# Second experts: outputs read back before the last three tiles, which are added by scatters to rows of their own

## The reference, cut to what matters

```python
def _L1_ffn_ref(x, w_fc, w_proj, w_gate):          # x: layer norm of h; H, NE, K = 768, 8, 2
    router_probs = softmax(einsum('btc,ce->bte', x, w_gate))
    top_p, top_i = top_k(router_probs, K)
    top_p = top_p / sum(top_p)
    ...  # h = gelu(x @ w_fc[:, :, e]), o = h @ w_proj[:, :, e] for the two experts e in top_i
    return einsum('btck,btk->btc', o, top_p)
h = h + _L1_ffn_ref(_layernorm(h), ...)
```

## Time and profile before

| | |
|---|---|
| median of the runs | 588.76 us |
| the profiled execution | 594.99 us, its span 593.2 us |
| TensorE | 492.7 us busy (83%) |
| VectorE | 319.5 us (54%) |
| ScalarE | 206.6 us (35%) |
| GpSimd | 154.6 us (26%) |
| DMA | 84.86 MB, mean 143 GB/s |

### The profile page before, as it was taken

One profiled execution on the slowest core, in us unless ns is written; L12 is line 12 of the kernel. 1 busy time (PEld: TensorE's weight loads), 2 busy tenths in 40 slices (PEclk: granted clock), 3 DMA queues, 4 the chain that ended last, 5 costly groups with the idle time before them and its releaser, 6 DMA issues.

```text
span 593.2 us, 12427 instructions
## 1 busy us (share of the span) xinstructions
PE 492.7 (83%) x4370; PEld 456.0 (77%) x4371; DVE 319.5 (54%) x1037; ACT 206.6 (35%) x441; POOL 154.6 (26%) x148
## 2 busy tenths in 40 slices
PE   3999999988514676899999679768999999999960
PEld 3999997568513565899999666758999999999950
DVE  1567999778999887322222466793222222222207
ACT  3630013857993357044343152261111121211110
POOL 1493000000001000555533300006544434443120
PEclk9999999989557667799999889879999999999995
DMA  8995100000006422387775497023666556667018
GB/s 302 411 339 152 51 1 1 0 3 2 0 1 220 129 106 108 84 217 179 180 171 109 108 277 306 1 107 98 202 204 184 168 166 187 183 183 209 28 52 294
DMA packets 40659, 84.86 MB, mean 143 GB/s; under 512 B 7270, under 2 KB 23186, under 8 KB 39586
## 3 DMA queue, kind: packets, MB, share of 16 engines
q1 hardware_dynamic: 33218, 72.81, 38.1%
q0 software_dynamic: 7392, 11.41, 8.5%
HBM read 70.33 MB, written 13.86 MB: 142 GB/s over the span
## 4 chain that ended last, share of the span: by engine, by line
PE 69%; DVE 17%; DMA 5%; ACT 4%; issue 2%; SPq 1%; POOL 0%; ACTq 0%; DVEq 0%; POOLq 0%
PE ps L1136 19%; PE ps L1112 13%; PE ps L886 13%; PE ps L1120 7%; DVE h L1923 2%; PE ps L1001 2%; DMA arena<-tok_w 1%; PE ps L1103 1%; PE ps L973 1%; DVE xT L1770 1%; PE ps L974 1%; PE ps L866 1%; PE ps L867 1%; DVE arena L1624 1%; DVE arena L1485 1%
## 5 line engine op out<-in xcount | busy, mean ns | idle before, releaser
L1136 PE MATMUL ps<-arena,xn 128*128 x696 | 123.1, 327 | 2.1 <-ACT xn L776 2.1
L1136 PEld LDWEIGHTS ps<-arena,xn 128*128 128x128 f32 x696 | 111.8, 190 | 4.2 <-issue 3.9
L514 POOL DMA_INDIRECT xT<-rows,from_i x58 | 56.3, 971 | 164.0 <-DVE from_i L1784 118.9
L886 PE MATMUL ps<-arena 128*128 128x192 f32 (+1 forms) x588 | 85.4, 333 | 10.2 <-DMA arena<-x_strips 9.2
L529 POOL DMA_INDIRECT made<-xT,to_i x58 | 67.9, 1170 | 99.2 <-DVE xT L1822 65.7
L886 PEld LDWEIGHTS ps<-arena 128*128 128x128 f32 (+1 forms) x588 | 83.3, 194 | 10.9 <-ACT arena L555 8.9
L1112 PE MATMUL ps<-xn,arena 128*128 128x128 f32 x696 | 88.0, 277 | 0.0
L1112 PEld LDWEIGHTS ps<-xn,arena 128*128 128x128 f32 x696 | 86.1, 194 | 0.1
L779 ACT ACTIVATE xn<-ps 128x384 f32<-128x384 f32 x78 | 32.6, 493 | 141.3 <-PE ps L1122 114.9
L1810 DVE COPY xn<-ps 128x128 f32<-128x128 f32 x58 | 16.9, 292 | 117.2 <-PE ps L1104 114.8
L776 ACT ACTIVATE xn<-ps,b_all 128x128 f32<-128x128 f32 x114 | 30.8, 390 | 62.6 <-PE ps L1122 51.0
(11 more groups left out here) (373 smaller groups left out, 771.1 us busy)
## 6 DMA issues: line engine op xcount, KB each, us to landing
arena<-ffn_a SPq DMA_DIRECT2D x58, 384.0 KB, 3.9
arena<-ffn_b SPq DMA_DIRECT2D x116, 96.0 KB, 4.4
arena<-x_blocks SPq DMA_DIRECT2D x16, 384.0 KB, 6.7
arena<-x_strips SPq DMA_DIRECT2D x3, 1536.0 KB, 12.3
arena<-ffn SPq DMA_DIRECT2D x4, 1152.0 KB, 15.5
rows<-xn SPq DMA_DIRECT2D x8, 384.0 KB, 2.3
arena<-made SPq DMA_DIRECT2D x8, 384.0 KB, 6.2
arena<-tok_w SPq DMA_DIRECT2D x8, 288.0 KB, 7.4
```

The source lines that it names most:

```text
L514: pool.indirect_dma_start(sx[:, k % 6], None, F["src"], bass.IndirectOffsetOnAxis(from_i[:, k:k + 1], 0)).then_inc(sem(f"sx_in{k % 6}"), 16)
L886: mm = pe.matmul(sum_ps(name, j), xs[rows, strip, 2 * j + b, 128 * c:128 * c + 128], w[rows], start=(name, j // 2) not in opened, stop=lef ...
L1136: mm = pe.matmul(ps[:, result_bank(k, N), 0:DIM], hT[:, u % 2, 128 * c:128 * c + 128], F["w2"][:, bass.ds(e2 + DIM * c, DIM)], start=(c == ...
```

## The change

`LATE = 3`. The rows of `made1` are set to zero early in the program, and the readback of all 4096 rows waits only for the scatters of tiles 0 to 35. The last three tiles (36, 37, 38) don't go to `made1`, so their rows read as zeros. Their results are multiplied by the row's share on VectorE as they leave PSUM, and scattered with addition to `late`: the first 2048 + 256 rows of `made0`, free by then, set to zero in the middle of F1; the row is the token's number (`late_i`). A token can have both of its rows in these tiles, so each of the three scatters waits until the one before has landed. `late` is then read in 4 pieces and added to h, each addition for four token blocks, and h is stored in 4 pieces. The shares of the late rows are gathered from DRAM, where a DMA puts `pk` (now laid out token, then choice) in the middle of F1. The buffer of the readback moves in SBUF, since the down weights of F1 are still in use when it fills. Some semaphores are shared by events that had one each (`ones_row`, `gate_set` and `wnat_set` become `pool_set`, `tok_b_in` becomes `cst_in`, `b2_in` becomes `ffn_in0`).

```diff
-STORES = ((0, 4), (4, 8), (8, 12), (12, 14), (14, 16))
+STORES = ((0, 4), (4, 8), (8, 12), (12, 16))
+LATE = 3
+        late = made0[0:TOKS + 256, :]
+        shares = rows0.rearrange("r (c o) -> (r c) o", o=1)
-        got = [h[:], view(0, [2 * NTOK, DIM])]
+        lin_at = E1 * HCH * DIM
+        got = [h[:], view(lin_at, [2 * NTOK, DIM])]
+        got_late = view(lin_at + 2 * NTOK * DIM, [NTOK, DIM])
...
+            sp.wait_ge(sem("pool_set"), 2)
+            sp.dma_start(made1[0:2 * TOKS, :].rearrange("(k p) c -> p k c", p=128),
+                         pbc[:, 0, :].unsqueeze(1).to_broadcast([128, 2 * NTOK, DIM])).then_inc(sem("made_set"), 16)
...
+                    if n and k == 12:
+                        late_set()
+            def late_set():
+                sp.wait_ge(sem("shares"), 1)
+                sp.dma_start(shares[0:2 * TOKS, :].rearrange("(p k) c -> p (k c)", p=128),
+                             pk[:].rearrange("p t s -> p (t s)")).then_inc(sem("shares_out"), 16)
+                sp.wait_ge(sem("pool_set"), 6)
+                sp.dma_start(late[0:TOKS + 128, :].rearrange("(k p) c -> p k c", p=128),
+                             pbc[:, 0, :].unsqueeze(1).to_broadcast([128, NTOK + 1, DIM])).then_inc(sem("made_set"), 16)
...
-                    sp.wait_ge(sem(f"y_st{n}{u}"), 16 * ((F["tiles"] + 2 - u) // 3))
+                    sp.wait_ge(sem(f"y_st{n}{u}"), 16 * ((F["tiles"] - LATE * n + 2 - u) // 3))
...
+            for u in range(3):
+                sp.wait_ge(sem(f"y_st1{u}"), 16 * ((TILES1 + 2 - u) // 3))
+            for i in range(4):
+                r = slice(4 * i, 4 * i + 4)
+                sp.wait_ge(sem("h_sum"), i + 1)
+                sp.dma_start(got_late[:, r, :], late[0:TOKS, :].rearrange("(b t) c -> b t c", t=NTOK)[:, r, :]).then_inc(sem(f"back_{i}"), 16)
...
-                for k in range(N):
+                pool.wait_ge(sem("made_set"), 64)
+                for k in range(N - LATE * n):
...
+                    if n and k == 14:
+                        pool.wait_ge(sem("shares_out"), 16)
+                        for x in range(LATE):
+                            pool.indirect_dma_start(share[:, x:x + 1], None, shares,
+                                                    bass.IndirectOffsetOnAxis(to_i[:, N - LATE + x:N - LATE + x + 1], 0)
+                                                    ).then_inc(sem("share_in"), 16)
             exchange(F0)
+            pool.memset(pbc[:, 0, :], 0.0).then_inc(sem("pool_set"), 1)
             exchange(F1)
+            pool.wait_ge(sem("made_set"), 80)
+            for k in range(TILES1 - LATE, TILES1):
+                pool.wait_ge(sem("y_out1"), k + 1)
+                if k > TILES1 - LATE:
+                    pool.wait_ge(sem(f"y_st1{(k - 1) % 3}"), 16 * ((k - 1) // 3 + 1))
+                pool.indirect_dma_start(late, bass.IndirectOffsetOnAxis(late_i[:, k - TILES1 + LATE:k - TILES1 + LATE + 1], 0), yo[:, k % 3],
+                                        None, compute_op=ALU.add).then_inc(sem(f"y_st1{k % 3}"), 16)
...
+            dve.wait_ge(sem("made_set"), 32)
             row, top = pbc[r3, 1, :], low[r3, 0, 0:96].bitcast(BF16)
...
+                if n:
+                    tail = slice(N - LATE, N)
+                    link(dve.tensor_scalar(pad, row[:, tail], -0.75, cst[:, C_P + 1:C_P + 2], ALU.is_lt, ALU.mult))
+                    dve.tensor_tensor(late_i[:], from_i[:, tail], pad, ALU.add)
...
+            def weighted(start, end):
+                for i in range(start, end):
+                    dve.wait_ge(sem(f"back_{i}"), 32 if i < 4 else 16)
+                    for s in range(2):
+                        for t in range(2 * i, 2 * i + 2):
+                            ins = dve.scalar_tensor_tensor(h[:, t, :], got[1][:, 2 * t + s, :], pk[:, t, s:s + 1], h[:, t, :], ALU.mult, ALU.add)
...
+                        ins = dve.tensor_scalar(yo[:, u % 3], ps[:, result_bank(k, N), 0:DIM], share[:, x:x + 1], None, ALU.mult)
...
+                        if n and isinstance(k, int) and k + 3 == N:
+                            dve.wait_ge(sem("share_in"), 16 * LATE)
+                            weighted(0, (0, 0, 1)[b])
                         result(k + b, u + b, j)
...
+            weighted(1, 8)
+            dve.wait_ge(sem("h_sum"), 8)
+            for i in range(4):
+                dve.wait_ge(sem(f"back_{i}"), 48)
+                r = slice(4 * i, 4 * i + 4)
+                dve.tensor_tensor(h[:, r, :], h[:, r, :], got_late[:, r, :], ALU.add).then_inc(sem("h_final"), 1)
```

More of the change, by code:

```diff
@@ L183, in build @@
         te_i = sb("te_i", [1, 4, 40], I32)
-        pk = sb("pk", [128, 2, NTOK])
+        pk = sb("pk", [128, NTOK, 2])
+        late_i = sb("late_i", [128, LATE], I32)
+        share = sb("share", [128, LATE])
+        late = made0[0:TOKS + 256, :]
+        shares = rows0.rearrange("r (c o) -> (r c) o", o=1)
         xnf = xn[:].rearrange("p a b -> p (a b)")
@@ L478, in link @@
                 pool.wait_ge(sem("pool_step"), steps[0])
[L481 to L482 removed]
+            pool.memset(xT1[K1:128, :], 1.0).then_inc(sem("pool_set"), 1)
+            pool.wait_ge(sem("pool_set"), 1)
             link(pool.memset(wnat[96:128, 5:7, :], 0.0))
+            link(pool.memset(pbc[:, 0, :], 0.0))
             for w in gate_w1:
[L485 to L487 removed]
+                pool.memset(w[K1:128], 0.0).then_inc(sem("pool_set"), 1)
+            pool.memset(wnat[64:128, 4, :], 0.0).then_inc(sem("pool_set"), 1)
+            pool.wait_ge(sem("pool_set"), 4)
             pool.wait_ge(sem("w_row"), 1)
@@ L1463, in _ @@
             token_row(1)
-            dve.wait_ge(sem("wnat_set"), 1)
+            dve.wait_ge(sem("pool_set"), 4)
             dve.wait_ge(sem("wnat_in"), 128)
@@ L1794, in route @@
                 dump, none = rt[:, 1280:1280 + N], g
+                pad = rt[:, 1324:1324 + LATE]
                 link(dve.tensor_scalar(dump, cst[:, C_TILE:C_TILE + N], 128.0, cst[:, C_P + 1 + n:C_P + 2 + n], ALU.mult, ALU.add))
                 link(dve.scalar_tensor_tensor(none, row, -0.75, dump, ALU.is_lt, ALU.mult))
+                if n:
+                    tail = slice(N - LATE, N)
+                    link(dve.tensor_scalar(pad, row[:, tail], -0.75, cst[:, C_P + 1:C_P + 2], ALU.is_lt, ALU.mult))
+                    dve.tensor_tensor(late_i[:], from_i[:, tail], pad, ALU.add)
                 dve.scalar_tensor_tensor(to_i[:, 0:N], row, 0.5 * n, none, ALU.add, ALU.add).then_inc(sem("places"), 1)
                 if n:
-                    dve.wait_ge(sem("soft_exp"), 1)
+                    dve.wait_ge(sem("exp_out"), 2)
                     link(dve.tensor_scalar(c16, d16, 1.0, None, ALU.add))
-                    link(dve.reciprocal(pk[:, 0, :], c16))
-                    dve.tensor_tensor(pk[:, 1, :], d16, pk[:, 0, :], ALU.mult)
+                    link(dve.reciprocal(pk[:, :, 0], c16))
+                    dve.tensor_tensor(pk[:, :, 1], d16, pk[:, :, 0], ALU.mult).then_inc(sem("shares"), 1)
+            def weighted(start, end):
[4 more added lines that the diff above has]
+                            ins = dve.scalar_tensor_tensor(h[:, t, :], got[1][:, 2 * t + s, :], pk[:, t, s:s + 1], h[:, t, :], ALU.mult, ALU.add)
+                        if s == 0:
+                            link(ins)
+                    ins.then_inc(sem("h_sum"), 1)
             def copies(F):
@@ L1820, in result @@
                         ins = dve.tensor_tensor(yo[:, u % 3], ps[:, result_bank(k, N), 0:DIM], b2_all[:, bass.ds(e, DIM)], ALU.add)
+                    elif isinstance(k, int) and k >= N - LATE:
+                        x = k - N + LATE
+                        ins = dve.tensor_scalar(yo[:, u % 3], ps[:, result_bank(k, N), 0:DIM], share[:, x:x + 1], None, ALU.mult)
                     else:
@@ L1892, in _ @@
             link(dve.tensor_tensor(ltmp[:, 0:16], ps[:, 6, 0:16], cst[:, C_SEL:C_SEL + 16], ALU.mult))
-            dve.tensor_reduce(stat[:, 500:501], ltmp[:, 0:16], AX.X, ALU.add).then_inc(sem("gate_logit"), 1)
+            dve.tensor_reduce(stat[:, 500:501], ltmp[:, 0:16], AX.X, ALU.add).then_inc(sem("exp_in"), 1)
             plus_normed(12, 16)
-            dve.wait_ge(sem("gate_exp"), 1)
+            dve.wait_ge(sem("exp_out"), 1)
             link(dve.tensor_scalar(stat[:, 502:503], stat[:, 501:502], 1.0, None, ALU.add))
@@ L1918, in _ @@
             copies(F1)
-            for i in range(8):
-                dve.wait_ge(sem(f"back_{i}"), 32 if i < 4 else 16)
-                for s in range(2):
-                    for t in range(2 * i, 2 * i + 2):
-                        ins = dve.scalar_tensor_tensor(h[:, t, :], got[1][:, 2 * t + s, :], pk[:, s, t:t + 1], h[:, t, :], ALU.mult, ALU.add)
-                    if s == 0:
-                        link(ins)
-                ins.then_inc(sem("h_final"), 1)
+            weighted(1, 8)
[4 more added lines that the diff above has]
```

(1 more changed line is left out.)

40 lines of the change are left out of this document (19 added, 21 removed).

## The result

The changed kernel is slower: its median is 598.78 us (four runs, 595.76 to 600.19) against 589.88 for the kernel before (four runs); the ratio on record is 1.0107 with a 95% interval of 1.0062 to 1.0152. Run again later, twelve times, it gave 1.0093 [1.0064, 1.0121], or 5.5 us, against 592.29 for 35 runs of the kernel before (588.74 to 595.64). The forecast was 591.0 us with a range up to 594.8. The ratios are the record's own and are not the quotients of the medians, which would be 1.0151 and 1.0110; the runs of one kernel spread over 6 to 8 us, so I go by the ratios and their intervals.

A forecast was written before the change was run, and what follows sets the result against it. The matrix engine holds 69% of the chain, but only the last 20 us can move: 7 us hidden, a serial late chain added, span 595.4 against 593.2. 588.76 + 2.2 = 591.0 us, range 587.5 to 594.8.

The forecast's parts named there:

- step 2: End chain: three adding scatters in a row, first 6.4 us, then 3.5 each; sum taken 14.0, bounds 11.1 to about 17.
- The base: The 2.2 us difference of spans was put on 588.76 us, the median of the runs of the kernel before.
- What goes: End: readback waits only for tile 35's scatter and the weighted additions end earlier, a gain of 7 us were nothing added.
- Step 1, the start: New end chain starts with tile 36's scatter at 569.67; multiplying by the share instead of copying was charged nothing.
- Steps 3 to 5, readback, addition, store: End: late readback of four pieces 7.05 us, last addition 0.96, last store 3.2, then 0.4 to the end.
- Saturated: End transfers saturate: first scatter 7.8 us, second 5.3, last store 4.7; 595.7 us, chance 0.18.
- Hardly felt: End scatters hardly feel the readback, 3.5 us each, store lands in 2.7; -1.2 us, 587.6 us, chance 0.17.
- short end: In addition to hardly felt, late readback lands 1.3 us sooner, store in 1.9; -3.3 us, 585.5 us, chance 0.06.
- VectorE keeps GpSimd out: End: 28 back-to-back two-input additions block generation of scatters 37 and 38 until 583.4; 598.0 us, chance 0.06.
- Weights of tile 12: Second experts: matrix engine waits for tile 12's weights behind the second zeroing, 3 us on top of 2.2; 594 us, chance 0.05.

The follow-up runs named there:

- b2: Changed kernel without its late path (three adding scatters, late readback, last four additions); the last three tiles' results are left out of the output: ratio 0.9887, tail 17.1 us.
- a2: Changed kernel without the two zeroings and the waits for them; output sums rows not set to zero: ratio 1.0051 against the kernel before, tail 27.9 us.
- a1: The changed kernel run once more with no edit: ratio 1.0093 against the kernel before, tail 28.5 us.
- a3: Changed kernel without the chain of waits, each late tile adding to rows of its own, only one set read back: ratio 0.9954, tail 21.3 us.
- a4: Changed kernel with readback pieces 4 to 7 held until tile 36's scatter has landed: ratio 1.0079 against the kernel before, tail 27.4 us.
- c2: Changed kernel with two sets of late rows, both read back, and readback pieces 4 to 7 held until tile 36's scatter landed: ratio 1.0017, tail 25.9 us.
- c1: Changed kernel with tile 37 adding to a second set of rows, tile 38 waiting for tile 36's scatter alone, both sets read back: ratio 1.0057, tail 26.6 us.
- b3: Changed kernel with two late tiles instead of three, weighted additions all behind the last result: ratio 1.0053 against the kernel before, tail 26.1 us.
- b4: Changed kernel with its three late scatters writing instead of adding, the chain of waits kept: ratio 1.0032 against the kernel before, tail 25.5 us.
- b1: Kernel before with only the two zeroings, the settings of the zero row and the waits for them added: ratio 0.9999, tail 24.2 us.
- c3: Changed kernel with one late tile instead of three, so no chain of scatters: ratio 1.0041 against the kernel before, tail 27.1 us.

## Why the prediction was wrong

Two terms failed: the landing of the first late scatter in step 2, and the base that the forecast was added to. I go through its own steps, taken from tile 36's result to the end of the span. The forecast for this stretch was 26.5 us, measured were 28.8.

- **What goes: right.** The readback left 2.4 us behind tile 35's scatter, and the additions were hidden. Worth 7 by the forecast, 6.7 by b2's ratio.
- **Step 1, the start: 0.4 too low.** From tile 36's result to its scatter's issue took 1.18 us, before 0.76. The multiplication by the share costs hardly more than the copy, as assumed (0.42 against 0.36 us); the rest goes with the added wait on GpSimd. In a2, where that wait is gone and the multiplication stays, it is 0.70.
- **Step 2, three scatters: the step that failed, 2.9 too low.** The first was taken at 6.4 us by the row with the nearest share of busy engines, and took 8.20 (7.96 and 7.93 in a1 and a2). This is above even the upper bound of 7.8. The share was no guide: over the three scatters of 5.3, 6.4 and 7.8 us it was 0.91, 0.93 and 0.93. And the one of 7.8, issued at 310.38, had no packet moved for its first 5.3 us, which the trace of before could have shown. The rows with 5.3 to 7.8 lay beside loads of weights, this one beside eight pieces of 384 KB issued within 3.7 us. The two gaps between a landing and the next issue were taken at 0.3 us and took 0.75 and 0.72, 0.9 together. The quiet scatters, 3.5 each, were right (3.66 and 3.56). The sum of the step, 16.9, lies within its own bounds (11.1 to about 17), but the range of the forecast did not carry them along.
- **Steps 3 to 5, readback, addition, store: 0.9 too high.** Forecast 11.7 us from the third landing to the end, measured 10.8: the late readback with its issue took 5.5 and not 7.1, the additions behind its last piece 1.9 and not 0.96, the store with what follows 3.3 and not 3.6.
- **The sum.** 0.4 + 2.9 - 0.9 gives 2.4 more than forecast, 2.3 measured. It makes 4.5 us of tail against before; the ratio says 5.5 (3.8 to 7.2 by its interval). The 1.0 between them isn't explained, and lies inside the interval.
- **The base.** The forecast was put on 588.76, the median of three runs. In 35 runs the median is 592.29. That is 3.5 us, more than the error of the sum, and the range had nothing in it for this. The error of the sum alone would have left the time at 593.3, within the range. The 7.8 us between 591.0 and the measured median of 598.78 are 3.5 of base, 2.3 of the sum, the unexplained 1.0, and 1.0 by which the medians (598.78 and 592.29) differ more than the ratio says.

The rivals. *Saturated* was the nearest: it had the first scatter at 7.8 and the cause, the full transfer beside it, and asked 6.9 of tail where 4.5 came, since it let the second scatter and the store suffer too, which they didn't. *Hardly felt* and *short end* are refuted by 8.20. *VectorE keeps GpSimd out* is refuted: GpSimd took 1.69 and 1.56 us for its scatters in the middle of and behind 28 additions back to back, and 1.61 for the one ahead of them; in a3, with both beside them, 1.58 and 1.56. The rule of the Trainium skill, SBUF — State Buffer, section Who interferes with whom, had no effect here that these rows show. *Weights of tile 12* is refuted by the matrix engine's busy time, 163.00 of 163.00. Its sum has a slip: 10.6 us grown by half from 437.3 give 453.2, 0.1 too late, not 453.8.

The first scatter again. The rows show three sizes for one adding scatter of 98 KB: 3.6 with nothing beside it, 4.0 and 4.3 beside what is left of half a readback (a4, c2), 6.8 to 8.2 beside a full one; 5.9 and 6.5 beside four pieces issued with it (c1, a4) lie between. That the readback makes it long is shown (a4), and that it doesn't have to run to its end first (b3). That the time goes in front of and between its packets and not in them is shown by the queues (1.2 MB first, then 76 ns a packet against 107 alone), and b4's writing scatter took 7.17 too, so reading back for the addition isn't most of it. What holds the first packet back that long, these runs don't show.

The Trainium skill, DMA: Bandwidth & Descriptors, section Queues, rings and completion order, has the engines take turns between queues by packet. Once the scatter's packets have begun, both queues do run side by side (186 and 144 packets from 571.34 to 574.60). But the prediction drew from it that the scatter waits for a packet or two and could be nearer 5, and said that the trace agrees. It does not: 442 packets of the readback came first, some 28 on each engine, and the measured 8.20 decides against the size. The scatter of 310.38 had told as much before the change.

## What to carry to other kernels

Moving a transfer ahead of its last inputs pays only if what finishes those inputs is short and not serial: here 7 us were hidden and 11.7 paid, of which having each adding scatter wait for the one before made 7.5 to 8.2. Price a small indirect transfer beside a deep readback at twice what it takes alone (7 to 8 us for 3.6 here), even though it doesn't wait for the readback's end, and look in the view of the queues when its first packet moves; holding part of the readback back only hands the delay to the next link of the chain. And before a forecast of half a per cent is put on a median, look at how far the runs spread: three were too few here by more than the effect.

## What the runs showed of the hardware that was not expected

**The same stretches take one of a few lengths.** The kernels are identical up to the second experts but for the small parts named, and yet the stretch of the first experts, from the first gather to the readback, took 97.0 us in before, a2, a3 and b4 (96.7 and 96.8 in c1 and c2), and 95.0 to 95.2 in after, a1, a4, b1, b2, b3 and c3. The stretch behind it, to the first store of normed rows, took 48.7 to 49.2, 50.3 to 50.6 or 52.4 to 52.8. The windows show what differs: the granted clock, first of before, then of after, at the same two places.

```profile
245.00:255.00 10.00, 9.74 (x85) 9.20 (x84) 2.29 (x9) 3.01 (x12) 5.27 (x6) 0.85 0.56 164
345.00:355.00 10.00, 6.90 (x46) 6.58 (x45) 5.39 (x37) 4.39 (x10) 0.00 (x0) 0.83 1.07 264
```

```profile
244.63:254.63 10.00, 9.74 (x97) 9.23 (x96) 2.65 (x10) 3.29 (x13) 5.29 (x6) 1.00 0.75 193
343.00:353.00 10.00, 7.53 (x65) 7.08 (x64) 6.45 (x41) 4.81 (x11) 0.00 (x0) 1.00 1.08 272
```

In before the clock was at its upper level for only part of these windows, in after for all of them, and in the first place as many busy us hold 85 matmuls in the one and 97 in the other. This is why the two profiled spans differ by 0.8 us only (593.2 and 594.0) although the tail is 4.5 longer: after's execution had got 3.7 back earlier. It is probably part of why twelve runs of one kernel spread over 6 to 8 us: over the 35 runs of before the time goes with the mean granted clock at a correlation of -0.5, over the twelve of a1 at -0.75. And it is why here a tail tells more than a span. What decides which length comes was not tried.

**One more wait on GpSimd goes with 0.4 to 0.5 us** ahead of an indirect transfer: 0.70 us from result to issue with one wait (a2), 1.18 with two; and the chained scatters, with two waits each, left 0.72 to 0.76 us behind the landing in all these executions. That the time goes with the number of waits, not with their kind, was not tried apart.
